# Edge loop of a four-layer graph network: filter product in three rounded parts, first layer two groups ahead

## The reference, cut to what matters

```python
xs, xv = x[:, :C] @ W_in2f_s, einsum('nci,cf->nfi', x[:, C:], W_in2f_v)     # per node, 128 + 3*128 wide
sj, vj = xs[idx_j], xv[idx_j]                                              # gathered per edge
h = softplus(f_ij @ Wf1 + bf1) - log(2)                                    # 20 -> 128, per edge
W = (h @ Wf2 + bf2) * rcut_ij[:, None]                                     # 128 -> 512 of it are used
m = concatenate([s2 * W[:, :2*F], v2 * W[:, 2*F:4*F], ...])                 # messages, 1024 wide here
agg = segment_sum(m, idx_i)                                                # summed per node
```

## Time and profile before

| | before |
|---|---|
| median of three runs | 2580.64 us |
| profiled execution, its own time | 2578.91 us |
| its span, first to last instruction | 2577.2 us |
| TensorE products busy | 2291.4 us, 89% |
| VectorE busy | 1690.3 us, 66% |
| GpSimd busy | 1375.3 us, 53% |
| ScalarE busy | 922.8 us, 36% |

### The profile page before, as it was taken

The page is one execution under the profiler, slowest core; times in us unless marked ns, Lnnn a source line. Parts: engine busy times, 40 slices in busy tenths (PEclk is TensorE's granted clock), DMA queues, the critical chain, the costliest instruction groups (busy, mean ns, idle before and its releaser), DMA issues.

```text
span 2577.2 us, 38097 instructions
## 1 busy us (share of the span) xinstructions
PE 2291.4 (89%) x7759; PEld 1176.1 (46%) x7759; DVE 1690.3 (66%) x4905; ACT 922.8 (36%) x2623; POOL 1375.3 (53%) x1706
## 2 busy tenths in 40 slices
PE   5789088727779999999998999999999999999997
PEld 3457067616655554454444333333333333333335
DVE  8973389939970421104136888888888888888885
ACT  0010077727760000000103444444444444444444
POOL 3886777776666666566504444444444444444440
PEclk7666555656669999999998999999999999999999
DMA  5212100011121211111102333333333333333331
GB/s 194 53 34 50 6 7 2 2 15 15 15 50 23 50 17 15 51 15 15 47 0 92 89 87 86 86 86 86 86 86 86 86 86 86 86 86 86 86 85 40
DMA packets 77939, 146.95 MB, mean 57 GB/s; under 512 B 28688, under 2 KB 41221, under 8 KB 77517
## 3 DMA queue, kind: packets, MB, share of 16 engines
q0 software_dynamic: 51200, 103.93, 17.6%
q1 hardware_dynamic: 23746, 37.13, 4.4%
q10 hardware_dynamic: 2946, 5.28, 0.6%
HBM read 122.74 MB, written 22.82 MB: 56 GB/s over the span
## 4 chain that ended last, share of the span: by engine, by line
PE 70%; POOL 15%; DVE 7%; issue 5%; DMA 2%; DVEq 1%; ACT 0%; ACTq 0%; SPq 0%; POOLq 0%
PE ps L747 25%; POOL pair_table L446 15%; PE ps L735 13%; PE ps L550 10%; PE ps L575 7%; PE ps L736 4%; PE ps L692 3%; PE ps L637 2%; PE ps L719 1%; DVE dense L1108 1%; DVE adj_t L1130 1%; DMA pair_table<-dense 1%; DVE dense L1107 1%; PE ps L669 1%; PE ps L727 1%
## 5 line engine op out<-in xcount | busy, mean ns | idle before, releaser
L747 PE MATMUL ps<-adj_t 128*128 128x512 f32 x1408 | 670.7, 609 | 0.0
L458 POOL DMA_INDIRECT src_table<-st_rec,st_idx x320 | 386.4, 1208 | 273.3 <-DMA st_rec<-records 181.2
L446 POOL DMA_INDIRECT pair_table<-dense x320 | 395.2, 1235 | 150.4 <-issue 96.6
L505 POOL DMA_INDIRECT adj_t<-z_table,adj_t x352 | 340.6, 968 | 182.3 <-issue 85.1
L927 ACT ACTIVATE adj_t<-adj_t 128x128 f32<-128x128 f32 x1056 | 343.3, 388 | 257.6 <-DVE adj_t L1275 257.6
L735 PE MATMUL ps<-wring,adj_t 128*128 128x512 f32 x704 | 371.8, 610 | 2.9 <-DVE adj_t L1249 2.9
L747 PEld LDWEIGHTS ps<-adj_t 128*128 128x128 f32 x1408 | 246.6, 190 | 251.0 <-issue 242.0
L636 PE MATMUL ps<-dense 128*128 128x128 bf16 x512 | 147.0, 287 | 188.4 <-DVE adj_t L1130 119.6
L637 PE MATMUL ps<-dense 128*128 128x128 f32 x1024 | 303.7, 434 | 0.0
L637 PEld LDWEIGHTS ps<-dense 128*128 128x128 f32 x1024 | 249.5, 299 | 19.5
L861 ACT ACTIVATE dense<-dense 128x128 f32<-128x128 bf16 x512 | 157.2, 307 | 248.9 <-DVE dense L1108 238.5
(11 more groups left out here) (208 smaller groups left out, 3083.3 us busy)
## 6 DMA issues: line engine op xcount, KB each, us to landing
src_table<-dense SPq DMA_DIRECT2D x8, 704.0 KB, 7.0
adj_t<-src_table SPq DMA_DIRECT2D x88, 64.0 KB, 1.8
adj_t<-z_table,adj_t POOLq DMA_INDIRECT x352, 3.6
pair_table<-dense POOLq DMA_INDIRECT x320, 2.6
src_table<-st_rec,st_idx POOLq DMA_INDIRECT x320, 2.6
records<-dense SPq DMA_DIRECT2D x1, 5000.0 KB
st_rec<-records POOLq DMA_DIRECT2D x80, 62.5 KB, 2.2
wring<-in_edge_attr SPq DMA_DIRECT2D x2, 1562.5 KB
```

The lines of the kernel that those rows point to most:

```text
L446: g.indirect_dma_start(out=pair_tables[h], out_offset=bass.IndirectOffsetOnAxis(ap=rows_i[h][0:EP, j:j + 1].bitcast(u32), axis=0), in_=pai ...
L458: g.indirect_dma_start(out=src_table, out_offset=bass.IndirectOffsetOnAxis(ap=st_idx[0:EP, k, c:c + 1].bitcast(u32), axis=0), in_=st_rec[0 ...
L505: g.indirect_dma_start(out=zg[:, s, c, :], out_offset=None, in_=z_table, in_offset=bass.IndirectOffsetOnAxis(ap=dsti[:, s, c:c + 1].bitcas ...
L747: last = mm(bank[6 + h], oh[:, c, :], msg[:, c, h * D:(h + 1) * D], start=c == 0, stop=c == GROUP - 1)
```

## The change

filter_out's one 32-bit product becomes three products of the rounded 32-bit type (float32r): the hidden values are split into a high part h_hi (ScalarE, hidden_hi) and a low part h_lo (GpSimd, hidden_lo), the weights into wf2_hi and wf2_lo once before the loop. The hidden values h32 themselves are single-buffered. The attributes' split, transposes, first layer and softplus are run two groups ahead rather than one, and the orders on TensorE, ScalarE, GpSimd and VectorE change with it. The core of the diff:

```diff
@@ gpsimd @@
+            def hidden_lo(i, s):
+                gi = 2 * i + s
+                wait_alone(pool, hi_ready, gi + 1)
+                if not (isinstance(gi, int) and gi < 2):
+                    wait_alone(pool, filt_done, GROUP * (gi - 1))
+                g.tensor_tensor(h_lo[:, s, :], h32, h_hi[:, s, :], ALU.subtract).then_inc(lo_ready, 1)
+
+            def group(i, s, one=True, two=True):
                 nxt = (i, 1) if s == 0 else (i + 1, 0)
-                for c in range(GROUP):
-                    if c < 2:
-                        gather(i, s, c + 2)
-                    elif not tail:
-                        gather(*nxt, c - 2)
+                gather(i, s, 2)
+                gather(i, s, 3)
+                if two:
+                    split(i + 1, s)
+                if one:
+                    hidden_lo(*nxt)
+                    gather(*nxt, 0)
+                    gather(*nxt, 1)
@@ tensor: filter_out @@
                 if c == 0:
-                    pe.wait_ge(h_ready, 2 * i + s + 1)
+                    pe.wait_ge(hi_ready, 2 * i + s + 1)
+                    pe.wait_ge(lo_ready, 2 * i + s + 1)
...
-                mm(bW[c], hT[:, s, c * P:(c + 1) * P], wf2_sb, start=True, stop=False)
+                mm(bW[c], h_hi[:, s, e], wf2_hi, start=True, stop=False)
+                mm(bW[c], h_hi[:, s, e], wf2_lo, start=False, stop=False)
+                mm(bW[c], h_lo[:, s, e], wf2_hi, start=False, stop=False)
@@ tensor: group @@
                 filter_out(i, s, 2)
-                if not tail:
-                    attrs_T(*nxt)
                 scatter(i, s, 0)
-                if not tail:
-                    filter_in(*nxt)
+                if two:
+                    attrs_T(i + 1, s)
                 filter_out(i, s, 3)
                 scatter(i, s, 1)
+                if two:
+                    filter_in(i + 1, s)
                 scatter(i, s, 2)
@@ scalar @@
+            def hidden_hi(i, s):
+                gi = 2 * i + s
+                act.wait_ge(h_ready, gi + 1)
+                if not (isinstance(gi, int) and gi < 2):
+                    act.wait_ge(filt_done, GROUP * (gi - 1))
+                A(h_hi[:, s, :], h32, ACT.Copy).then_inc(hi_ready, 1)
+
                 c_part(i, s, 0)
-                if not tail:
-                    attrs(*nxt)
+                if one:
+                    hidden_hi(*nxt)
+                if two:
+                    attrs(i + 1, s)
                 c_part(i, s, 1)
-                if not tail:
-                    softplus_exp(*nxt)
                 c_part(i, s, 2)
-                if not tail:
-                    softplus_log(*nxt)
+                if two:
+                    softplus_exp(i + 1, s)
                 c_part(i, s, 3)
+                if two:
+                    softplus_log(i + 1, s)
@@ vector @@
             deinterleave(wf2_sb, wf2_raw)
+            link(v.tensor_copy(wf2_hi, wf2_sb))
+            link(v.tensor_tensor(wf2_lo, wf2_sb, wf2_hi, ALU.subtract))
...
                 dve.wait_ge(sp_ready, gi + 1)
-                if not (isinstance(gi, int) and gi < 2):
-                    dve.wait_ge(filt_done, GROUP * (gi - 1))
-                v.scalar_tensor_tensor(hT[:, s, :], bank[1], 0.0, sp, ALU.max, ALU.add).then_inc(h_ready, 1)
+                if not (isinstance(gi, int) and gi == 0):
+                    dve.wait_ge(hi_ready, gi)
+                    dve.wait_ge(lo_ready, gi)
+                v.scalar_tensor_tensor(h32, bank[1], 0.0, sp, ALU.max, ALU.add).then_inc(h_ready, 1)
...
                 v.scalar_tensor_tensor(vy[:, c, :], vk[1], y[1], vy[:, c, :], ALU.mult, ALU.add).then_inc(vy_chain, 1)
+                if nxt:
+                    hidden(*nxt)
                 dve.wait_ge(filt_done, n + 1)
...
-                if nxt:
-                    hidden(*nxt)
...
-                messages(i, s, 0)
+                messages(i, s, 0, nxt=None if tail else (i if s == 0 else i + 1, 1 - s))
```

More of the change, by code:

```diff
@@ L72, in build @@
           l2_w, l2_b, w_in_s, w_in_v, wf1, bf1, wf2, bf2, w1_s, w1_v, w2_s, w2_v, out):
-    f32, bf16, i32, u32 = mybir.dt.float32, mybir.dt.bfloat16, mybir.dt.int32, mybir.dt.uint32
+    f32, f32r, bf16, i32, u32 = mybir.dt.float32, mybir.dt.float32r, mybir.dt.bfloat16, mybir.dt.int32, mybir.dt.uint32
     ALU, ACT, AX = mybir.AluOpType, mybir.ActivationFunctionType, mybir.AxisListType
@@ L94, in build @@
         adj = adj_t[:, :].rearrange("p (k n) -> p k n", k=2)
-        dense = sb("dense", [P, NT * D + 2 * KT * N])
+        with nc.sbuf_tensor("dense", [P, NT * D + 2 * KT * N], f32) as dense:
+            pass
+        dense_r = sb("dense_r", [P, NT * D + 2 * KT * N], f32r)
         xb = dense[:, 0:NT * D].rearrange("p (t n) -> p t n", t=NT)
@@ L195, in build @@
         aT = carve(P, 2 * MSG).rearrange("p (s m n) -> p s m n", s=2, m=8)
+        wf2_hi, wf2_lo = [dense_r[:, NT * D + 2 * N + k * D:NT * D + 2 * N + (k + 1) * D] for k in range(2)]
+        h_hi, h_lo = [dense_r[:, NT * D + KT * N + 2 * k * D:NT * D + KT * N + 2 * (k + 1) * D].rearrange("p (s n) -> p s n", s=2) for k in range(2)]
         svT = T1[:, 1, 0:2 * D].rearrange("p (s n) -> p s n", s=2)
@@ L477, in split @@
                 gi = 2 * i + s
+                wait_alone(pool, rec_in[s], 16 * (i + 1))
                 if not (isinstance(gi, int) and gi < 2):
@@ L506, in gather @@
                                      in_offset=bass.IndirectOffsetOnAxis(ap=dsti[:, s, c:c + 1].bitcast(u32), axis=0)).then_inc(z_in[s][c], 16)
[L508 to L515 removed]
+            def hidden_lo(i, s):
[5 more added lines that the diff above has]
+            def group(i, s, one=True, two=True):
+                nxt = (i, 1) if s == 0 else (i + 1, 0)
+                gather(i, s, 2)
[6 more added lines that the diff above has]
+                    gather(*nxt, 1)
             pool.wait_ge(full, first["l2_agg"] + NT)
             g.memset(agg, 0.0).then_inc(agg_zero, 1)
+            split(0, 0)
+            split(0, 1)
             gather(0, 0, 0)
             gather(0, 0, 1)
+            hidden_lo(0, 0)
             group(0, 0)
@@ L525, in _ @@
                 group(i, 1)
-            group(L3_IT - 1, 0)
-            group(L3_IT - 1, 1, tail=True)
+            group(L3_IT - 1, 0, two=False)
+            group(L3_IT - 1, 1, one=False, two=False)
         @block.tensor
@@ L748, in scatter, with group @@
                 last.then_inc(scat_chunk, 1)
-            def group(i, s, tail=False):
+            def group(i, s, one=True, two=True):
                 nxt = (i, 1) if s == 0 else (i + 1, 0)
                 filter_out(i, s, 2)
-                if not tail:
-                    attrs_T(*nxt)
                 scatter(i, s, 0)
-                if not tail:
-                    filter_in(*nxt)
+                if two:
+                    attrs_T(i + 1, s)
                 filter_out(i, s, 3)
                 scatter(i, s, 1)
+                if two:
+                    filter_in(i + 1, s)
                 scatter(i, s, 2)
-                if not tail:
+                if one:
                     filter_out(*nxt, 0)
                 scatter(i, s, 3)
-                if not tail:
+                if one:
                     filter_out(*nxt, 1)
@@ L769, in _ @@
             pe.wait_ge(l3w_ready, 2)
-            attrs_T(0, 0)
-            filter_in(0, 0)
+            for s in range(2):
+                attrs_T(0, s)
+                filter_in(0, s)
             filter_out(0, 0, 0)
@@ L948, in _ @@
             softplus_log(0, 0)
+            attrs(0, 1)
+            hidden_hi(0, 0)
+            softplus_exp(0, 1)
+            softplus_log(0, 1)
             group(0, 0)
@@ L1304, in group @@
                     one_hot(i, s, c)
-                    messages(i, s, c, nxt=(i if s == 0 else i + 1, 1 - s) if c == GROUP - 1 and not tail else None)
+                    messages(i, s, c)
             hidden(0, 0)
```

5 lines of the change are left out of this document (3 added, 2 removed).

## The result

The changed kernel takes 2588.24 us (median of 6 runs, 2586.66 to 2591.70), the kernel before beside it 2580.84 us (6 runs): a ratio of 1.0032, interval 1.0021 to 1.0042. It is slower by 0.3%, where 0.6% faster was forecast; the time lies inside the range given. The profiled execution took 2588.09 us.

The account below looks back on a forecast made before the run. A TensorE queue without gaps was taken to bound the edge loop. 86 x -0.19 = -16.5 us, +2 at the start, -2 at the end, turned 2578.91 into 2562.4, median 2564 us; 8-in-10 range 2540 to 2605.

Parts of the forecast that it names:

- the stall before scatter 1: TensorE between transposes and scatter 1: stands still 0.71 us a group while a 1.98 us chain runs through ScalarE.
- Rival 1: TensorE at scatter 1: no stall, period 11.91 us, 2500 us in all; chance 0.07.
- the step of the product: TensorE's filter products: each rounded 512-column product takes 0.215 us, one pass, with its weight load hidden.
- the whole forecast gain of 0.19: Edge loop: period falls from 12.81 to 12.62 us a group.
- rival 2: TensorE's filter products: each rounded product pays for its weight load; 2580 to 2603 us, or 2642 at 0.10 us; chance 0.13.
- the cover at scatter 0: VectorE's chain from scatter 1 ends at 8.36 us, TensorE reaches scatter 0 at 8.8: 0.4 us of cover.
- rival 3: VectorE becomes late, held by GpSimd or late gathers, once 0.4 us is lost; mostly 2570 to 2590 us; chance 0.12.
- the parts at nothing: hidden_hi, hidden_lo (1.2 us on GpSimd), gathers and weight preparation: hidden behind other work, costing nothing.
- The start: Before group 0's first filter product: waits for hidden_hi and hidden_lo, +2 us.
- the end: Last two groups have no transposes, so they keep the 0.85 us saving: -2 us.
- VectorE waits for Ln at hidden: VectorE before hidden, ahead of a group's first message work: waits nearly 2 us a group, free while the covers last.
- Rival 4: TensorE's filter products: rounded type not run in one pass, 0.43 us each; about 2730 us; chance 0.08.

Follow-up runs that it names:

- e3: The changed kernel with attrs on ScalarE moved behind c_part of chunk 1; 2538.08 us, ratio 0.9832 to the kernel before.
- e12: The changed kernel complete, with the first layer's steps back at their old places on TensorE and Exp and Ln one c_part earlier; ratio 0.9794 to the kernel before.
- e1: The kernel before in its own order, three rounded products replacing the 32-bit product, low part left out; 2524.86 us, ratio 0.9780 to the kernel before.
- e11: As e1, but each rounded product cut into two of 256 columns with the same weights; single run 2620.11 us, 0.994 of the kernel before.
- e4: The changed kernel with VectorE's register read of the sums' place moved to the group's start; 2584.29 us, ratio 1.0014 to the kernel before.
- e6: The changed kernel with the three products on bf16 operands, same order; ratio 1.0036 to the kernel before.
- e10: The changed kernel with bf16 products and the register read moved to the group's start, together; ratio 0.9930 to the kernel before.
- e2: The changed kernel with one plain 32-bit product in place of the three rounded ones; 2625.73 us, ratio 1.0171 to the kernel before.
- e7: The changed kernel with hidden_lo cut to 4 of 512 columns and the high part used in the third product; ratio 1.0032 to the kernel before.
- e5: The changed kernel with the edits of e3 and e4 together; ratio 0.9930 to the kernel before.

## Why the prediction was wrong, point by point

**Right: the stall before scatter 1.** The mechanism and its price held. T to scatter 1 takes 1.99 to 2.08 us (forecast 1.98); the stall is 0.53 to 0.62 (forecast 0.71, less because filter product 3 took longer). e3 removed it and e12 avoided it. Rival 1 is refuted. Only the name in the profile differed: "issue", not ScalarE.

**Wrong: the step of the product, 0.215 taken, 0.233 measured.** This term was mis-sized: L756 to L757 is 0.23 or 0.24 us. Filter products 0 to 2 take 1.11, 1.12 and 1.22 us against 1.045, 1.045 and 1.125, 0.235 more a group, of which 9 x 0.018 = 0.16 is the step. The 0.235 is more than the whole forecast gain of 0.19. In e1, where nothing else is in the way, the products save 0.64 us a group, where the forecast had 0.85. The step is close to the break-even that rival 2 named (0.021 us a product), but the mechanism of rival 2 is not this one: the loads are hidden, and the time goes with the columns (e11). TensorE: Matmul & The Clock Gate of the Trainium skill, section "The mechanism", has a weight load overlap running products only when its row group differs, and by that each full-row load would wait for the product before it. The 0.118 us steps of e11, six loads of 0.19 us among them, speak against that here.

**Wrong: the cover at scatter 0, 0.4 us taken, none there.** Counted from the start of scatter 1, in the longer of the two kinds of group:

| step of the VectorE chain | forecast, us | changed kernel, us |
|---|---|---|
| to the start of hidden (Ln done) | 5.15 | 4.99 |
| hidden | 0.61 | 0.61 |
| L1316 to the addition's start | 1.38 | 2.19 |
| the addition L1335 | 1.22 | 1.22 |
| to scatter 0 | 0 | 0.15 |
| sum; scatter 0 in TensorE's order | 8.36; 8.8 | 9.16; 9.0 |

The error is in the third row, 0.81 us, of which 0.73 is the register read; the first and the last row cancel to 0.01. The prediction put nothing between L1285 and the addition, and gave no reason, though in the earlier trace rows the addition has the same 0.73 us in front, put down to TensorE's scatter. It was the read, with a semaphore wait behind it that had been met: with the read moved (e4) the idle time goes, and the wait is still in the code. The totals agree: L1296 waited 47.0 us over 70 groups before, and L1335 waits 47.1 us over 70 now, although everything around it has moved. The effect at scatter 0 is small all the same, 0.15 us in one kind of group and 0.03 in the other, because TensorE itself comes there at 9.0 instead of 8.8. That is rival 3 (VectorE late, decided at 0.4 us lost at scatter 0), by a cause it did not name: neither GpSimd nor a gather.

**How the two combine.** The period is the sum of two chains that leave TensorE's filter products out: scatter 1 to scatter 0 through ScalarE and VectorE (9.16), scatter 0 (1.79), T to scatter 1 through ScalarE (2.07): 13.02, the long group. So e6 with its faster products gained nothing (12.92), and e4 without the read gained only 0.09 us a group (12.83), because TensorE's own 9.0 to scatter 0 stood next. Only both mended give 12.59 (e10). In e3 the last term is 1.39 instead of 2.07, and the period falls by 0.6. The same sum explains e2: three plain products are 3 x 0.15 us longer, so TensorE's own path to scatter 0 is 9.46, longer than VectorE's 9.16, scatter 0 takes 1.82 without a wait, and 9.46 + 1.82 + 2.07 is 13.35 (13.28 and 13.35 alternate, mean 13.32). So of the 0.64 us a group that the products save in e1, the changed kernel loses about 0.15 (filter product 3, under the stall) and about 0.1 (behind VectorE at scatter 0). That is 0.25 us a group, or 21 us, against the 18 us missing in the times above.

**The range.** The time lies inside 2540 to 2605, but that does not bear out the sum. The centre was 24 us off, and the change went the other way. Rival 2's own sum at 0.02 us a product gives 2580; the measured time is 8 us above it, and no rival joined the slower step with the late addition.

**Right: the parts at nothing.** hidden_lo took 1.28 us (1.2 taken) and costs nothing (e7; in e12 it lies in a loop without gaps). The start grew by 2.2 us (T of group 0 to its first product 5.81 before, 8.01 now; +2 forecast), and the end gave back about 2. VectorE waits for Ln at hidden, 70.9 us over 70 groups, 1.0 us each; I had said nearly 2. The 0.67 us a group of the read, which I had left out, is the larger part of the difference; I have not accounted for the rest. Rival 4 (two-pass rate) is refuted by the steps of 0.233.

## What to carry to other kernels

Before work is moved past a queue, write out every chain between the engines, and keep every gap in it until it is shown that it goes. A gap of the same length in group after group can be the waiting engine's own instruction, whatever engine the profile names; here it was a register read, and moving that one line showed it. When a transpose moves, look at what the next engine has queued behind the copy-out of its result: the new order cost 45 us with the old product (e2), and moving one step behind another on ScalarE gave 50 us back (e3). And when TensorE's products get cheaper, look for what else is then as long as its path; here VectorE's chain stood up to 0.15 us beyond it.

## What the hardware showed that was not expected

- One product of 512 columns follows the other in 0.233 us in the rounded 32-bit type (0.118 for 256 columns), in 0.216 us in bf16 (e6), both at a granted clock of 1.00. Why the rounded type is 8% slower stays open.
- A register read on VectorE costs it 0.55 to 0.73 us within a group; just behind the loop's start the gap with the read is 1.15 us (e5), without it 0.29. No instruction shows it, only "issue", or the engine of the next wait.
- VectorE's L1297, whose operands (a 32-bit matrix and two columns) lie in SBUF, took 1.22 us beside GpSimd's 1.28 us subtraction and 0.34 elsewhere (e4). SBUF — State Buffer of the Trainium skill, "SBUF: two separate sides", has GpSimd hold the shared port for its whole instruction; the two ends, 1908.11 and 1908.19, agree with it. In the changed kernel the subtraction falls beside L1335 instead, and no L1297 takes over 0.54 us, so e7 does not show what this hold costs. In e4 scatter 1 comes 1.99 to 2.08 us after T, as without the hold.
